# The sum of squares of the gated output: column matmuls against ones, or two transposes and a VectorE sum

## The reference, cut to what matters

```python
o = gla_chunk_scan(q * SCALE, kn, v, rt_log) + shift * residual_weight   # [16, 512, 512]
xg = o * jax.nn.silu(final_gate)
rms = jax.lax.rsqrt(jnp.mean(xg * xg, axis=-1, keepdims=True) + NORM_EPS)
o = xg * rms * norm_weight
return o @ down_w.T                                                      # [16, 512, 256]
```

## Time and profile before

| | us |
|---|---|
| median of three runs | 1938.95 (1938.80 to 1940.89) |
| the profiled execution | 1940.21 |
| its span, first to last instruction | 1938.40 |
| TensorE matmul busy | 1921.8 (99% of the span) |
| VectorE busy | 1584.1 (82%) |
| ScalarE busy | 1295.3 (67%) |
| GpSimd busy | 81.2 (4%) |
| granted TensorE clock, mean | 0.998 |

### The profile page before, as it was taken

The page is one execution under the profiler, slowest core; times in us unless marked ns, Lnnn a source line. Parts: engine busy times, 40 slices in busy tenths (PEclk is TensorE's granted clock), DMA queues, the critical chain, the costliest instruction groups (busy, mean ns, idle before and its releaser), DMA issues.

```text
span 1938.4 us, 46120 instructions
## 1 busy us (share of the span) xinstructions
PE 1921.8 (99%) x16804; PEld 1902.9 (98%) x16804; DVE 1584.1 (82%) x4304; ACT 1295.3 (67%) x2687; POOL 81.2 (4%) x136
## 2 busy tenths in 40 slices
PE   8999999999999999999999999999999999999998
PEld 7999999999999999999999999999999999999998
DVE  7788888888788887888888788787888878888887
ACT  5666667767676766666766667675667666667575
POOL 0000000000000000000000000000000000000000
PEclk9999999999999999999999999999999999999999
DMA  8000000000000000000000000000000000000000
GB/s 309 7 12 13 12 2 12 12 12 12 13 1 12 13 12 12 8 5 13 12 13 12 7 6 12 13 12 13 1 12 13 12 12 12 1 13 12 13 7 8
DMA packets 23538, 34.19 MB, mean 18 GB/s; under 512 B 3170, under 2 KB 19810, under 8 KB 23364
## 3 DMA queue, kind: packets, MB, share of 16 engines
q1 hardware_dynamic: 23364, 31.43, 4.8%
HBM read 23.04 MB, written 8.39 MB: 16 GB/s over the span
## 4 chain that ended last, share of the span: by engine, by line
PE 94%; issue 2%; ACT 1%; DVE 1%; SPq 1%; DMA 0%; POOLq 0%; POOL 0%; DVEq 0%; ACTq 0%
PE fb L383 64%; PE ab L383 21%; PE ab L593 2%; PE ab L628 1%; PE ab L529 1%; PE ab L453 1%; PE ab L518 1%; PE ab L583 1%; PE fb L678 1%; SPq L289 0%; PE ab L590 0%; PE ab L469 0%; PE ab L606 0%; ACT wwhole L726 0%; DMA sgate<-stage_w 0%
## 5 line engine op out<-in xcount | busy, mean ns | idle before, releaser
L383 PE MATMUL fb<-hid1h,wwhole 128*128 128x256 f32 x2048 | 474.2, 279 | 0.1
L383 PE MATMUL fb<-hid1l,wwhole 128*128 128x256 f32 x2048 | 467.9, 276 | 0.0
L383 PE MATMUL fb<-hid0l,wwhole 128*128 128x256 f32 x2048 | 465.9, 276 | 0.0
L383 PE MATMUL fb<-hid0h,wwhole 128*128 128x256 f32 x2048 | 465.8, 276 | 0.0
L383 PEld LDWEIGHTS fb<-hid1h,wwhole 128*128 128x128 f32 x2048 | 384.5, 188 | 4.0 <-ACT raw L838 0.3
L383 PEld LDWEIGHTS fb<-hid1l,wwhole 128*128 128x128 f32 x2048 | 384.7, 188 | 0.0
L383 PEld LDWEIGHTS fb<-hid0h,wwhole 128*128 128x128 f32 x2048 | 384.5, 188 | 0.0
L383 PEld LDWEIGHTS fb<-hid0l,wwhole 128*128 128x128 f32 x2048 | 384.4, 188 | 0.0
L838 ACT ACTIVATE raw<-fb,sh_s 128x256 f32<-128x256 f32 x512 | 212.3, 465 | 150.3 <-PE fb L383 142.7
L383 PE MATMUL fb<-xntl,wwhole 128*128 128x256 f32 x1024 | 237.5, 276 | 0.0
L383 PE MATMUL fb<-xnth,wwhole 128*128 128x256 f32 x1024 | 237.5, 276 | 0.0
(11 more groups left out here) (234 smaller groups left out, 4481.6 us busy)
## 6 DMA issues: line engine op xcount, KB each, us to landing
xin<-x SPq DMA_DIRECT2D x32, 256.0 KB, 2.7
out<-xin SPq DMA_DIRECT2D x32, 256.0 KB, 2.2
stage_more<-stage_w SPq DMA_DIRECT2D x6, 512.0 KB, 7.1
sgate<-stage_w SPq DMA_DIRECT2D x4, 512.0 KB, 4.4
shift<-stage_w SPq DMA_DIRECT2D x4, 512.0 KB, 5.0
v<-stage_w SPq DMA_DIRECT2D x4, 512.0 KB, 5.6
raw<-stage_w SPq DMA_DIRECT2D x3, 512.0 KB, 6.0
mixed<-stage_w SPq DMA_DIRECT2D x3, 512.0 KB, 8.2
```

The costliest lines, as they stand in the source:

```text
L383: mm = pe.matmul(o, a, b, start=start and i == 0, stop=stop and i == len(pairs) - 1)
```

## The change

ScalarE squares in two pieces of two feature blocks each, and each piece has its signal. VectorE adds block 1 to block 0 and block 3 to block 2 in place as the pieces come, waits for both, and adds the two results into `sqsum`, in place of one reduction. TensorE, at the same place behind the down product, transposes the two 128 x 128 blocks of `sqsum` into `fb[1]` (columns 0 to 255) in place of the two products against ones. VectorE sums each block of 128 columns of `fb[1]` into a new tile `total`, waits for that, and makes the mean from it. Waits elsewhere, and the order of all other lines, stay as they are. The signal counts are adjusted.

```diff
-        msq, rms = sb("msq", [P, NC]), sb("rms", [P, NC])
+        msq, rms, total = sb("msq", [P, NC]), sb("rms", [P, NC]), sb("total", [P, NC])
...
-        sq_d, xg_hi, ln_hi = sig("sq_d", 1), sig("xg_hi", 1), sig("ln_hi", 1, 1)
+        sq_d, xg_hi, ln_hi = sig("sq_d", 2), sig("xg_hi", 1), sig("ln_hi", 1, 1)
...
-        sqsum_d = sig("sqsum_d", 1)
+        sqsum_d, total_d = sig("sqsum_d", 4), sig("total_d", 1)
...
                 for c in range(NC):
-                    mm = pe.matmul(fb[1][:, c:c + 1], sqsum[:, c * CH:(c + 1) * CH], ones[:, 0:1], start=True, stop=True)
+                    mm = pe.transpose(fb[1][:, c * P:(c + 1) * P], sqsum[:, c * CH:(c + 1) * CH], ident_s[:])
                 mm.then_inc(rs_mm.sem, 1)
...
-                act.activation(sq[:], sgate[:], ACT.Square).then_inc(sq_d.sem, 1)
+                for d in (0, 2):
+                    act.activation(sq[:, d:d + 2, :], sgate[:, d:d + 2, :], ACT.Square).then_inc(sq_d.sem, 1)
...
-                dve.wait_ge(sq_d.sem, sq_d.at(me))
-                dve.tensor_reduce(sqsum, sq.rearrange("p d t -> p t d"), mybir.AxisListType.X, ALU.add).then_inc(sqsum_d.sem, 1)
+                for d in (0, 2):
+                    dve.wait_ge(sq_d.sem, sq_d.at(me, d // 2 + 1))
+                    dve.tensor_tensor(sq[:, d, :], sq[:, d, :], sq[:, d + 1, :], ALU.add).then_inc(sqsum_d.sem, 1)
+                dve.wait_ge(sqsum_d.sem, sqsum_d.at(me, 2))
+                dve.tensor_tensor(sqsum, sq[:, 0, :], sq[:, 2, :], ALU.add).then_inc(sqsum_d.sem, 2)
...
                 dve.wait_ge(rs_mm.sem, rs_mm.at(me))
-                dve.tensor_scalar(msq[:], fb[1][:, 0:NC], 1.0 / DI, EPS, ALU.mult, ALU.add).then_inc(msq_d.sem, 1)
+                dve.tensor_reduce(total[:], fb[1][:, 0:NC * P].rearrange("p (c k) -> p c k", c=NC), mybir.AxisListType.X,
+                                  ALU.add).then_inc(total_d.sem, 1)
+                dve.wait_ge(total_d.sem, total_d.at(me))
+                dve.tensor_scalar(msq[:], total[:], 1.0 / DI, EPS, ALU.mult, ALU.add).then_inc(msq_d.sem, 1)
```

## The result

The kernel with the change took **1946.46 us** (median of 9 runs, 1944.86 to 1948.85), the kernel before 1940.89 beside it (9 runs, 1938.80 to 1942.35): ratio 1.0033, 95% interval 1.0024 to 1.0041. It is slower by 5.6 us, where the prediction had 4.5 us less than before. Its profiled execution took 1948.85, its span is 1947.0; that of before had 1938.40. So the two traces lie 8.6 us apart, more than the medians do: the profiled run of the kernel after was the slowest of its nine.

A forecast was written before the change was run, and what follows sets the result against it. The prediction took the sum of TensorE's matmul starts to bound the kernel; -4.34 - 0.45 + 0.33 = -4.46 us from the 1938.95 median gave 1934.5 us, range 1933.3 to 1938.0.

The forecast's parts named there:

- TensorE, removed and added: Behind the down product, two transposes replace four one-column passes: 0.14 us less per half, -4.3 us over 31 halves.
- the floor of about 25 ns: Start-to-start minimum between matmuls; by it alone the four passes would cost 0.10 us and the change would lose, 1943.0.
- (b): Rival: first pass behind the transposes starts 0.15 us late in each half, +0.6 us in all, 1939.6; chance 8%.
- (c): Rival: one-column passes cost less than a weight load, so the transposes are dearer, +3.4 us, 1942.4; chance 6%.
- the term of -4.3 us: TensorE's saving at the joins: 31 halves times 0.14 us, bounds -3.7 to -4.7.
- The join itself: At TensorE's loop end, fewer recorded passes let its stream arrive earlier and reduce late starts: -0.45 us.
- the upper bound, +2.1: Case of the join where the loop end stays put while work shrinks: all 15 ends lose 0.14 us each.
- In the halves and at the joins between them TensorE waits for nobody: Basis of the forecast: no such wait rows, so time is the sum of TensorE's starts.
- More margin is worth nothing: Ahead of the transposes, the earlier VectorE sum gains nothing, since TensorE's load already had 1.06 us of margin.
- VectorE and ScalarE: Squares about 1.1 us, additions 0.415 each, new reduction 0.42; delays covered by idle time, costing nothing except behind the last half.
- The tail: Behind the last half, where VectorE's chain ends the program, the later mean costs +0.33 us once.
- Rival (a): The loop ends lose 2.1 us of the transposes' 4.34 gain, leaving -1.9 us, 1937.0; chance 12%.

The follow-up runs named there:

- e13: Kernel before with the later wait and reordered products, TensorE's code 96 instructions later and 60 memsets ahead on VectorE, without the change: 1941.29 us, ratio 1.0002.
- e14: The change with the later wait and reordered products, TensorE's code 96 instructions later, 60 VectorE memsets: 1938.17 us, ratio 0.9985 to the kernel before.
- e10: The change with the later wait and reordered products, and TensorE's code 96 instructions later: 1938.78 us, ratio 0.9991 to the kernel before.
- e7: The change with the wait for the input's low part 8 products later and the projections' low-part products last: 1939.76 us, ratio 1.0001 to the kernel before.
- e12: The change with the later wait and reordered products, TensorE's code 96 instructions later, 60 VectorE memsets: 1938.11 us, ratio 0.9992 to the kernel before.
- e3: The change with 34 warm-up matmuls written as 17 of twice the width, 34 instructions fewer ahead of the loop: 1972.86 us, ratio 1.0170 to the kernel before.
- e4: The kernel before with 34 warm-up matmuls written as 17 of twice the width, 34 instructions fewer ahead of the loop: 1989.95 us, ratio 1.0257.

## Why the prediction was wrong

**TensorE, removed and added: right.** 0.14 per half was forecast; 0.148 was measured at the join (e13, e14). The rule of the floor of about 25 ns that spoke against it, from the Trainium skill's "TensorE: Matmul & The Clock Gate", "Wait — 56ns, not 53.3ns?", does not decide here: in e13 only the second of the four passes starts 0.026 behind the first, the others 0.111. Rivals (b) and (c) are out as mechanisms. The half gave 0.05 of it back elsewhere, which no step had, so that the term of -4.3 us was nearer -3 (2.8 over 29 halves).

**The join itself: wrong, and it was the first step that failed.** "With the change that stream has two recorded passes to put through there in place of four, so it should reach the loop end earlier; then all 0.69 goes." The stream did reach the loop end earlier, by 0.6 us against the array, and nothing came of it, because what it waits for there is a transfer of instructions whose time hardly depends on it. The mechanism was that of the upper bound, +2.1. The traces have 2.2 us more lateness in place of -0.45, of which the late halves make up about half: what is left is some +1.1 (1.9 us from e10 to e7, 0.8 from e13 to before). The prediction's reading "it is TensorE's own instruction stream reaching the next half late" was true and stopped one question short: the branch's own durations, up to 1239 ns, were there to be read.

**"In the halves and at the joins between them TensorE waits for nobody": the step that cost most.** True by the views of waits, and not enough. In the p = 0 halves behind a loop end the wait for the low part held the first projection's load by 0.06 us, before the change as after it, and behind such a load TensorE has two paces, 113.3 and 117.8 ns. This loss (6.2 us by the ratios of after and e7, more than the whole slowdown) was in no rival. Why the change makes halves slow that were not slow before stays open. What I held to be impossible was a cost without a row of its own.

**"More margin is worth nothing": right in its effect, wrong in its reason.** The sequencer had no margin, and the earlier sum let it reach the loop end earlier (1.1 us ahead of the array with the late sum, 1.6 to 1.8 with the early one). The branch took that back.

**VectorE and ScalarE: each duration right** (reduction 0.42, addition 0.417, two squares 1.14 for 1.1), the cover as foreseen in both joins, no wait in the next half. What was missed is that more VectorE instructions move the code of the last sequence, where VectorE stood for its own instructions for 2.32 instead of 0.76 us: +2.0 in the trace.

**The tail: right.** +0.33 was forecast. From the first pass of the last L678 to the start of the last addition it is 1.97 in the traces without the change and 2.32 in those with it, +0.35. At the end of the span it can't be seen, since the rest, the store above all, differs by 0.5 us between traces of the same code there.

Rival (a) (1937.0) was the nearest in mechanism: it took place, and a second and third came on top. In number (c) was the nearest (1942.4), by luck, since its mechanism did not. The ratios to the kernel before put the parts in a row: same surroundings without the change 1.0002 (e13), with it 0.9985 (e14), the loop ends and the last sequence as they were 1.0001 (e7), the wait where it was 1.0033 (after). So the change itself is worth -0.17%, the loop ends and the last sequence cost 0.16%, the slow pace 0.32%; each step has an uncertainty of about 0.12%. How far such a row can be trusted shows in e12, the same kernel as e14 on another chip, at 0.9992: with it the middle step is 0.09%. Only e13 and e14 were run on one chip.

## What to carry to other kernels

An engine that is 99% busy can still be late: count its starts in equal windows, half by half, and compare the halves with fewer starts with the rest, before trusting that a view of waits without rows means no cost. In a kernel whose loop body has thousands of instructions (here some 2100 of TensorE), a change worth a tenth of a per cent can't be told from where it puts the code; run both kernels with the same few idle instructions ahead of the loop, at two or three places, and look at the duration of the backward branch (medians here from 357 to 3649 ns). And look at the start of the weight load behind a wait: one held by a few hundredths of a microsecond makes no row, and moving the wait a few products later gained 0.32% here with the change and nothing without it.

## What the hardware did that I had not expected

- The backward branch of TensorE, where it was taken, lasted 0.34 to 3.9 us, most of it decided by where the code lay; 34 instructions fewer ahead of the loop cost 33 us (e3) and 50 us (e4), 96 more made every loop end punctual.
- Two stable paces of the same matmuls at the same granted clock of 1.00: 113.3 and 117.8 ns from start to start, set where a wait held a weight load by 0.06 us, and kept for 33 us in most cases.
- A first pass through written-out code stopped VectorE for 0.8 to 2.3 us while 8 KB of instructions came, at a place that moved with the number of instructions.
- TensorE's sequencer was 1.1 to 1.8 us ahead of its array at the loop end, so that a semaphore counted as early by the array's clock was not early for it.
